# Value sums of a finished sequence placed among the scores of the next, and a layer's expert work cut into separate items

## The chip, the cores and the metric

The kernel runs on one core of one Trainium2 chip. The metric is device time in microseconds (us), the median of several executions of the same program. Inside the core the work is shared by TensorE (PE in the profile: matrix products and transposes), VectorE (DVE), ScalarE (ACT: exponentials, tanh, gelu, copies), GpSimd (POOL) and SyncE (SP: it issues the DMA transfers). Each engine takes its instructions strictly in the order in which the program gives them, and semaphores hold it where it needs another engine's result.

## The reference, cut to what matters

Four sequences of 512 tokens with 128 channels pass through four layers. Each layer normalizes x, computes a mixing branch s and a mixture of experts g from the normalized x, and adds `s * g` with g through a silu:

```python
x = L0_attn_x
for layer in (0, 1, 2, 3):
    xn = _layernorm(x, axis=-1)
    s = attn_ref(layer, xn)
    g = _silu(ffn_ref(layer, xn))
    x = x + s * g
```

The layers differ. Layer 0 is a selective scan with 8 experts. Layer 1 (the second layer, "causal") is causal attention with 16 heads of 8 channels, softmax with the row maximum taken out, and 4 gated experts that are ever used. Layer 2 (the third layer, "rope") is attention whose numerator uses rotated queries and keys and whose denominator uses the plain ones, so each score is computed twice, without maxima; its 8 experts have 64 hidden channels each. Layer 3 ("alibi") is attention with a distance bias and 16 routed experts. The change touches the order of work in layers 1 and 2.

## The kernel before, in words

`flow` builds one list of items for layers 1 to 3, written out as (what, layer, sequence, number). TensorE, ScalarE and VectorE all walk this list in `attention()` and do their own part of each item, so the list is the order on every one of them. SyncE has an order of its own, which the change leaves alone. The items are:

- `q`: one projection of the next sequence to queries or keys on TensorE, its copy out of the accumulator by ScalarE, and its split into three bf16 parts by VectorE (layer 2 has four of them); `v`: the values; `gate` and `cw`: the expert logits and, from them, the expert weights.
- `a`: a unit of scores (layers 1 and 3) of which VectorE takes the row maxima; `mx` turns the maxima, and SyncE writes them beside the queries.
- `b`: a unit of scores, 128 x 1024, of which ScalarE takes the exponential. Layer 1 has 20 of them a sequence, layer 2 has 64: 32 "plain" ones, whose exponentials are only summed (ScalarE takes two instructions of 512 columns, L1213), and 32 rotated ones (one instruction of 1024 columns, L1230). TensorE computes unit u when the exponential of unit u-2 is done, since the units share two pairs of accumulator banks.
- `pv`: one part of the value sums (L975), eight stages a sequence, each with one to three parts; the last part of four heads is followed by VectorE's copy (L1651), by `bc` (transposes on TensorE, L984, and the division by the denominator on VectorE, L1658).
- `f` in layer 1: an expert chunk. TensorE computes two products (`up`, L686 and L687), ScalarE a tanh (L1089), VectorE two products (`gated`, L1356 and L1360), and TensorE adds the chunk before it to the expert's output (`down`, L699). `up` of a chunk and all of `q`, `v`, `gate` and the transpose of `t` 3 use the accumulator bank MI, and each waits until the one before it has been read (`mi_read`).
- `f` in layer 2: `up` of two experts at once (L687), a gelu on ScalarE (L1094, with a table load before it and one behind it), and `down` of the chunk before it, which is two experts: the second expert's matmuls wait until VectorE (`mix`, L1382, four instructions) has read the first expert's output, since both use bank YB. `fl` is the last `down`; `mb` begins the mixture with the experts' biases (L666, L670).
- `t` 0 to 3, the tail of a sequence: transposes of the heads' output and ScalarE's copy (`t` 0, L990, L1248), the output projection (`t` 1, L996), VectorE's normalization, the combination with the experts and the next moments (`t` 2, L1678 to L1394), and the normalized x, its transpose (L651) and copy (`t` 3).

`schedule` gives a sequence's own items. In layer 1 it spreads the 22 expert chunks over `a` and `b`, and ends with the last value sums, the last chunk and `fl`; in layer 2 the last chunk and `fl` stand together before the last 16 items, and the last value sums stand at the end. `flow` then puts the tail of the previous sequence behind the items at `TAIL_AT` and the head items of the next sequence (`q`, `v`, `gate`, `cw`) behind those at `HEAD_AT`. So the end of one sequence of layer 2 and the beginning of the next read before:

```
... f3 fl b53 b54 b55 b56 b57 pv6.0 b58 pv6.1 b59 ... b63 pv7.0 pv7.1 bc3 |
    b0 b1 t0 b2 b3 t1 b4 b5 b6 t2 b7 ... b10 t3 b11 mb b12 b13 f0 pv0.0 b14 pv0.1 ...
```

Of the kernel before, what the change touches and what calls it, by code (L numbers as in the profile page):

```python
# [27 lines left out]
NB = 4  # L28
# [289 lines left out]
KIND = {1: "causal", 2: "rope", 3: "alibi"}  # L318
# [31 lines left out]
def schedule(l):  # L350
# [10 lines left out]
    a = [("a", u) for u in range(len(score_units(KIND[l])[0]))]  # L361
    b = b_items(KIND[l])
    if l == 1:
        return spread(a, f[:7]) + [("mx", 0)] + f[7:9] + spread(b, f[9:]) + [("fl", 0)]
    if l == 2:
        return b[:12] + [("mb", 0)] + b[12:14] + f[:1] + spread(b[14:-16], f[1:]) + [("fl", 0)] + b[-16:]
    return a + [("mx", 0)] + b
# [3 lines left out]

TAIL_AT = {1: (1, 4, 32, 47), 2: (1, 3, 6, 10), 3: (1, 3, 6)}
HEAD_AT = {1: (("q", 0, 36), ("q", 1, 40), ("v", 0, 44), ("gate", 0, 49), ("cw", 0, 52)),
           2: (("q", 0, 30), ("q", 1, 36), ("q", 2, 42), ("q", 3, 48), ("v", 0, 54), ("gate", 0, 58), ("cw", 0, 62)),
           3: (("q", 0, 8), ("q", 1, 12), ("v", 0, 16))}

# [5 lines left out]

def flow(layers):


    out, tail = [], []
    for l in layers:
        if not l:
            continue
        if l == 3:  # L390
            out += tail + [("route", l, 0, 0)]
            tail = []
        if l != 2 or l == layers[0]:
            out += tail + head_items(l, 0)
            tail = []
        for b in range(NB):
            after = {}
            for k, item in enumerate(tail):
                after.setdefault(TAIL_AT[l][k], []).append(item)
            if b + 1 < NB:  # L400
                for what, n, at_ in HEAD_AT[l]:
                    after.setdefault(at_, []).append((what, l, b + 1, n))
            elif l == 1 and 2 in layers:
                for k, item in enumerate(head_items(2, 0)):
                    after.setdefault(42 + 5 * k, []).append(item)
            for k, (what, n) in enumerate(schedule(l)):
                out.append((what, l, b, n))
                out += after.pop(k, [])
            assert not after, after
            tail = [("t", l, b, k) for k in range(len(TAIL_AT[l]) - (l == layers[-1] and l != 3))]  # L410
    return out + tail
# [1538 lines left out]
```

## Time and profile before

| | us |
|---|---|
| median of 3 executions | 2229.74 (2228.86 to 2235.36) |
| the profiled execution: its own time | 2235.12 |
| its span, first to last instruction | 2233.3 |
| TensorE busy | 1588.4 (71%) |
| VectorE busy | 1234.8 (55%) |
| ScalarE busy | 1040.8 (47%) |
| granted TensorE clock, mean share of full speed | 0.786 |

The second layer runs from about 625 to 1160 us of the span, the third from 1160 to about 1690, the fourth from there to the end. Busy shares are means over these stages, so they say little; what counts in a stage is which engine waits for which. TensorE's clock has two levels, 1.2 and 2.4 GHz, and a granted clock of 0.67 over a stretch means that it stood at the upper level for about a third of it.

### The profile page before, as it was taken

The page shows a single profiled execution, that of the slowest core. Times are in us where ns is not written, and L with a number is a line of the kernel's source. Part 1 is how long each engine was busy: PE and PEld are TensorE (multiplying, and loading weights), DVE is VectorE, ACT ScalarE, POOL GpSimd, SP SyncE. Part 2 cuts the span into 40 slices and gives each one's busy share as a digit, 9 for nine tenths or more (in the row PEclk, how much of TensorE's full clock was granted, in tenths as well). Part 3 has the DMA queues.
Part 4 walks back from the last instruction along what each step waited for, and adds up shares of the span by engine and source line. Part 5 has one row for each costly group of instructions (what it writes and reads, how often), then busy time and mean ns, then how long its engine had stood idle before and what let it go on. Part 6 is the DMA issues. An engine that isn't in the chain of part 4 may idle for free.

```text
span 2233.3 us, 24309 instructions
## 1 busy us (share of the span) xinstructions
PE 1588.4 (71%) x8520; PEld 786.7 (35%) x8520; DVE 1234.8 (55%) x2493; ACT 1040.8 (47%) x1569; POOL 222.0 (10%) x208
## 2 busy tenths in 40 slices
PE   5667657757679889797877767676674456877767
PEld 2444434434435445454442322222223042222222
DVE  4976958859765564746653324232215727455371
ACT  3856937748404133231336676576660031423415
POOL 0431413404200000000000000000000210000000
PEclk8987978878779999999996667576666575868768
DMA  5000000000111010010133203021001141111200
GB/s 220 1 1 0 0 0 0 0 0 0 35 55 52 8 44 15 2 50 8 30 86 111 71 17 97 15 78 36 1 1 43 39 113 41 55 41 37 56 22 6
DMA packets 73990, 83.09 MB, mean 37 GB/s; under 512 B 8764, under 2 KB 70716, under 8 KB 73276
## 3 DMA queue, kind: packets, MB, share of 16 engines
q1 hardware_dynamic: 72856, 79.60, 11.9%
q0 software_dynamic: 1024, 2.10, 0.3%
q8 instruction: 59, 0.97, 0.2%
q14 instruction: 51, 0.42, 0.1%
HBM read 50.47 MB, written 31.20 MB: 37 GB/s over the span
## 4 chain that ended last, share of the span: by engine, by line
PE 42%; DVE 29%; ACT 12%; issue 12%; DMA 2%; POOL 1%; SPq 1%; DVEq 0%; ACTq 0%; POOLq 0%
PE ps L975 9%; DVE neg_max L1638 7%; PE ps L699 6%; PE ps L687 5%; PE ps L686 4%; ACT scratch L1230 4%; DVE mixture_sum L1382 3%; ACT ps L1213 2%; DVE scratch L1486 2%; PE ps L845 2%; DVE gated L1356 2%; DVE hidden L1360 2%; PE ps L984 1%; DVE scratch L1475 1%; ACT tanh L1089 1%
## 5 line engine op out<-in xcount | busy, mean ns | idle before, releaser
L1230 ACT ACTIVATE scratch<-ps 128x1024 f32<-128x1024 f32 x336 | 335.2, 1021 | 290.1 <-PE ps L945 142.3
L1638 DVE TENSOR_REDUCE neg_max<-ps 128x2 f32<-128x1024 f32 (+2 forms) x224 | 224.5, 1064 | 20.8 <-PE ps L890 20.4
L975 PE MATMUL ps<-scratch,values 128*32 128x512 f32 (+3 forms) x1536 | 224.8, 671 | 15.7 <-ACT scratch L1230 10.1
L1651 DVE COPY head_out<-ps 128x512 f32<-128x512 f32 x48 | 33.1, 689 | 323.7 <-PE ps L975 323.6
L1811 POOL TENSOR_TENSOR scratch<-scratch 128x512 f32<-128x512 f32 x128 | 160.2, 1273 | 360.6 <-DVE scratch L1486 360.6
L1089 ACT ACTIVATE tanh<-ps 128x512 f32<-128x512 f32 x88 | 52.6, 597 | 291.9 <-PE ps L687 291.9
L699 PEld LDWEIGHTS ps<-weights_even,hidden 128*128 128x128 f32 (+1 forms) x960 | 148.0, 226 | 96.5 <-issue 53.7
L1213 ACT ACTIVATE ps<-ps 128x512 f32<-128x512 f32 x256 | 150.7, 589 | 63.9 <-PE ps L934 63.9
L699 PE MATMUL ps<-weights_even,hidden 128*128 128x128 f32 (+1 forms) x960 | 156.2, 315 | 33.5 <-DVE mixture_sum L1382 33.5
L1481 DVE TENSOR_TENSOR_SCAN scratch<-scratch 128x512 f32<-128x512 f32 x128 | 175.6, 1410 | 1.5 <-ACT scratch L1149 1.5
L687 PE MATMUL ps<-xnt_sequence,weights_even 128*128 128x512 f32 x256 | 149.5, 674 | 0.0
L1356 DVE SCALAR_TENSOR_TENSOR gated<-tanh,ps 128x512 f32<-128x512 f32 x88 | 60.4, 686 | 156.9 <-ACT tanh L1089 156.9
L1382 DVE SCALAR_TENSOR_TENSOR mixture_sum<-ps,combine,mixture_sum 128x128 f32<-128x128 f32 x304 | 85.2, 341 | 106.8 <-PE ps L699 106.8
L1094 ACT ACT_TABLE_LOAD x84 | 107.8, 1283 | 20.4 <-PE ps L699 19.0
L686 PE MATMUL ps<-xnt,weights_odd 128*128 128x512 f32 x176 | 107.9, 697 | 12.8 <-DVE hidden L1360 8.7
L1766 POOL TENSOR_SCALAR variance_eps<-mean_var 128x4 f32<-128x4 f32 x20 | 4.6, 228 | 1129.7 <-DVE mean_var L1279 1129.7
L750 PE MATMUL ps<-scratch 96*128 96x512 bf16 x128 | 42.7, 423 | 90.7 <-DVE scratch L1486 88.0
L699 PEld LDWEIGHTS ps<-weights_odd,hidden 128*128 128x128 f32 x640 | 87.4, 198 | 46.4 <-issue 40.7
L890 PE MATMUL ps<-scratch 52*128 52x256 bf16 (+7 forms) x704 | 103.6, 367 | 0.0
L934 PE MATMUL ps<-scratch 48*128 48x512 bf16 x256 | 72.6, 510 | 39.3 <-ACT ps L1213 38.4
L943 PE MATMUL ps<-scratch 48*128 48x512 bf16 x256 | 69.7, 517 | 41.6 <-ACT scratch L1230 34.8
L687 PE MATMUL ps<-xnt,weights_odd 128*128 128x512 f32 x176 | 97.7, 639 | 0.0
(268 smaller groups left out, 2545.4 us busy)
## 6 DMA issues: line engine op xcount, KB each, us to landing
scratch<-parts_scratch SPq DMA_DIRECT2D x288, 96.0 KB, 2.3
parts_scratch<-weights_even SPq DMA_DIRECT2D x192, 128.0 KB, 2.4
weights_odd<-in_l SPq DMA_DIRECT2D x1, 4224.0 KB, 28.2
weights_even<-in_l SPq DMA_DIRECT2D x1, 4096.0 KB, 17.2
weights_odd<-in_l SPq DMA_DIRECT2D x1, 4096.0 KB, 12.7
slots_scratch<-weights_even SPq DMA_DIRECT2D x2, 1280.0 KB, 6.3
scratch<-in_sel SPq DMA_DIRECT2D x1, 1024.0 KB, 6.4
slots_scratch<-xn SPq DMA_DIRECT2D x1, 1024.0 KB, 9.5
```

What stands on the lines that cost most here:

```text
L686: pe.matmul(ps[:, MI, :], W(l, "w3")[:, P * f:P * (f + 1)], src, start=True, stop=True)
L687: pe.matmul(ps[:, up_bank(l, f), :], w1, src, start=True, stop=True)\
L699: mm = pe.matmul(ps[:, YB, P * j:P * (j + 1)], buf[lo:lo + n, P * j:P * (j + 1)], W(l, "w2")[lo:lo + n, P * src:P * (src + 1)], start=(one ...
L975: mm = pe.matmul(ps[32 * i:32 * i + 32, PV, q0:q0 + n], lhs, buf[:, slot, col:col + n], start=first_, stop=True, skip_group_check=True)
L1094: act.activation(hidden_buffer(l, f), ps[:, up_bank(l, f), :], ACT.Gelu, bias=W(l, "b1")[:, f:f + 1])\
L1213: ins = act.activation(bank, bank, ACT.Exp, accum_out=dens[:, j, h:h + 1])
L1230: act.activation(dst, src, ACT.Exp).then_inc(q[l, "exp_done"], 1)
L1356: own.link(stt(act_g[:, :], act_t[:, :], 1.0, ps[:, UP, :], ALU.add, ALU.mult))
L1382: ins = stt(facc[:, j, :], yj, cw[:, j, e:e + 1], facc[:, j, :], ALU.mult, ALU.add)
L1481: dve.tensor_tensor_scan(l0["hs"][:, g, :], l0[f"da{s % 2}"][:, g, :], l0["ub"][:, g, :], 0.0, ALU.mult, ALU.add).then_inc(q[l, "da_free"], 1)
L1638: ins = dve.tensor_reduce(dst, ps[:, base:base + 2, col:col + n], AX.X, ALU.max, negate=True)
L1811: pool.tensor_tensor(l0["y"][:, g, :], l0["y"][:, g, :], l0["hc"][:, g, :], ALU.add)\
```

## The change

`schedule` no longer serves layers 1 and 2. New functions build each sequence:

- `split_late` takes the trailing `pv` and `bc` items off a sequence's list (layer 1: bc2, three parts of stage 6, stage 7, bc3; layer 2: stage 7 in two parts, bc3). `woven` puts them one at a time behind the first items of the next sequence, from its second item on, followed by `t` 0 and `t` 1 and, at distances filled with `None`, `t` 2 and `t` 3. This holds between the layers 1 and 2 too.
- In layer 1 the chunks 9 to 21 are spread over the shorter list, so they stand closer together, and the head items' places are counted in the new list.
- In layer 2 `mb` stands three items behind `t` 3, and each chunk gives three items, `f`, `dn` (f, 0) and `dn` (f, 1): the `up`, and each expert's `down` by itself with its `mix`. They are spread over the rest of the sequence.
- The items are the same in number and size but for that cut; the fourth layer's list is the same as before.

The same place in layer 2 reads after the change:

```
... b55 dn3.0 b56 b57 pv6.0 b58 dn3.1 pv6.1 b59 ... b63 |
    b0 b1 pv7.0 b2 pv7.1 b3 bc3 b4 t0 b5 t1 b6 ... b9 t2 b10 ... b13 t3 pv0.0 b14 pv0.1 mb b15 b16 b17
    pv1.0 b18 pv1.1 q0 f0 b19 bc0 b20 b21 b22 q1 dn0.0 b23 b24 b25 pv2.0 b26 q2 dn0.1 pv2.1 b27 ...
```

The middle of a sequence of layer 1, and its beginning, read before and after (x. marks items of the previous sequence, n. of the next):

```
before: mx f7 f8 b0 b1 b2 x.t2 b3 f9 b4 b5 n.q0 pv0.0 f10 b6 pv0.1 n.q1 b7 f11 pv0.2 b8 n.v pv1.0 f12 b9 x.t3
after:  mx f7 f8 b0 b1 b2 f9 b3 b4 x.t2 b5 f10 n.q0 pv0.0 b6 f11 pv0.1 n.q1 b7 pv0.2 f12 b8 n.v x.t3 pv1.0 b9 f13
before: bc2 pv6.0 pv6.1 f20 pv6.2 pv7.0 bc3 f21 fl | a0 a1 x.t0 a2 f0 a3 x.t1 a4 a5 f1
after:  f20 pv5.0 b19 f21 fl | a0 a1 x.bc2 a2 x.pv6.0 f0 x.pv6.1 a3 x.pv6.2 a4 x.pv7.0 a5 x.bc3 f1 x.t0 a6 x.t1
```

The diff, cut to its core:

```diff
-    if l == 1:
-        return spread(a, f[:7]) + [("mx", 0)] + f[7:9] + spread(b, f[9:]) + [("fl", 0)]
-    if l == 2:
-        return b[:12] + [("mb", 0)] + b[12:14] + f[:1] + spread(b[14:-16], f[1:]) + [("fl", 0)] + b[-16:]
-TAIL_AT = {1: (1, 4, 32, 47), 2: (1, 3, 6, 10), 3: (1, 3, 6)}
-HEAD_AT = {1: (("q", 0, 36), ("q", 1, 40), ("v", 0, 44), ("gate", 0, 49), ("cw", 0, 52)),
+def split_late(items):
+    n = len(items)
+    while items[n - 1][0] in ("pv", "bc"):
+        n -= 1
+    return items[:n], items[n:]
+def sequence1(b, late):
...
+    begin = spread(a, f[:7])
+    items, rest = split_late([(w, l, b, n) for w, n in b_items("causal")])
+    main = begin + [("mx", l, b, 0)] + f[7:9] + spread(items, f[9:]) + [("fl", l, b, 0)]
+    return woven(main, late, 1), rest
+def sequence2(b, late):
+    l = 2
+    items, rest = split_late([(w, l, b, n) for w, n in b_items("rope")])
+    items = woven(items, late + [None, None, ("mb", l, b, 0)], 1)
+    extra = []
+    for f in range(NF[l]):
+        extra += [("f", l, b, f), ("dn", l, b, (f, 0)), ("dn", l, b, (f, 1))]
+    first = items.index(("mb", l, b, 0)) + 2
+    return items[:first] + spread(items[first:-6], extra) + items[-6:], rest
+def woven(main, late, first):
+    late, out = list(late), []
+    for n, item in enumerate(main):
+        out.append(item)
+        if late and n >= first:
+            extra = late.pop(0)
+            out += [extra] if extra else []
+    return out + [item for item in late if item]
...
+HEAD_AT = {1: (("q", 0, 46), ("q", 1, 50), ("v", 0, 54), ("gate", 0, 59), ("cw", 0, 62)),
+           2: (("q", 0, 30), ("q", 1, 36), ("q", 2, 42), ("q", 3, 48), ("v", 0, 54), ("gate", 0, 60), ("cw", 0, 66)),
+def first_layers():
...
+            main, rest = (sequence1 if l == 1 else sequence2)(b, late)
...
+            t = [("t", l, b, k) for k in range(4)]
+            late = rest + ([t[0], t[1], None, None, None, t[2], None, None, None, t[3]] if l == 2 or b == NB - 1 else
+                           [t[0], t[1]] + [None] * 26 + [t[2]] + [None] * 9 + [t[3]])
...
-            def down(l, b, f):
+            def down(l, b, f, part=None):
...
-                for e, lo, n, src, one, last in DG[l][f]:
+                for e, lo, n, src, one, last in DG[l][f] if part is None else DG[l][f][part:part + 1]:
...
-                        if n:
+                        if l == 1 and n:
                             down(l, b, n - 1)
+                    elif what == "dn":
+                        down(l, b, n[0], n[1])
...
-            def mix(l, b, f):
+            def mix(l, b, f, part=None):
...
+                    elif what == "dn":
+                        mix(l, b, n[0], n[1])
```

## Rows read from the trace of the kernel before

**Rows 1.** The page: the span.

```profile
span 2233.3 us, 24309 instructions
```

**Rows 2.** Windows: a sequence of layer 1, one of layer 2.

```profile
core 0: us, PE busy (x) PEld busy (x) DVE busy (x) ACT busy (x) POOL busy (x), PEclk, DMA share, GB/s
760.00:895.00 135.00, 113.87 (x724) 62.64 (x722) 81.44 (x171) 36.18 (x48) 2.53 (x4) 0.95 0.09 25
...
1294.00:1424.00 130.00, 91.53 (x406) 33.87 (x406) 41.68 (x129) 87.22 (x183) 2.53 (x4) 0.68 0.17 49
```

**Rows 3.** Waits of ACT in 1290:1420, one sequence of layer 2: sum, times, longest.

```profile
ACT ps L1213 <- PE ps L934: 14.5, 9, 5.5
ACT scratch L1230 <- PE ps L943: 13.5, 6, 7.0
ACT xnt L1077 <- PE ps L651: 5.3, 1, 5.3
ACT weights_even L1200 <- PE ps L845: 4.5, 2, 3.7
ACT combine_second L1082 <- DVE combine L1314: 2.4, 1, 2.4
```

**Rows 4.** Timeline of ACT, layer 2: start, duration, in brackets the idle time before.

```profile
1318.69 1.94 ACT L1230 ACTIVATE scratch<-ps 128x1024 f32<-128x1024 f32 x2 [3.52 <-PE ps L943]
...
1403.12 1.02 ACT L1230 ACTIVATE scratch<-ps 128x1024 f32<-128x1024 f32 x1 [7.04 <-PE ps L943]
...
1423.32 0.58 ACT L1213 ACTIVATE ps<-ps 128x512 f32<-128x512 f32 x1 [6.21 <-PE ps L934]
```

**Rows 5.** Waits of PE in 1294:1424, layer 2.

```profile
PE ps L699 <- DVE mixture_sum L1382: 6.3, 5, 1.3
```

**Rows 6.** The page's costliest groups: the exponentials of the whole span.

```profile
L1230 ACT ACTIVATE scratch<-ps 128x1024 f32<-128x1024 f32 x336 | 335.2, 1021 | 290.1 <-PE ps L945 142.3
...
L1213 ACT ACTIVATE ps<-ps 128x512 f32<-128x512 f32 x256 | 150.7, 589 | 63.9 <-PE ps L934 63.9
```

**Rows 7.** Timeline of PE, layer 2, instructions at the upper clock.

```profile
1327.97 1.06 PE L975 MATMUL ps<-scratch,values 128*32 128x512 f32 x8
1328.96 0.39 PE L943 MATMUL ps<-scratch 48*128 48x512 bf16 x2
...
1391.38 1.12 PE L687 MATMUL ps<-xnt,weights_even 128*128 128x512 f32 x2
1392.43 1.16 PE L699 MATMUL ps<-weights_even,hidden 64*128 64x128 f32 x8
```

**Rows 8.** Timeline of PE, layer 2, instructions at the lower clock.

```profile
1316.04 2.07 PE L670 MATMUL ps<-weights_even,combine_t 8*128 8x128 f32 x8 [0.77 <-DVE combine_t L1348]
...
1365.79 2.08 PE L699 MATMUL ps<-weights_even,hidden 64*128 64x128 f32 x8
...
1405.48 0.61 PE L934 MATMUL ps<-scratch 48*128 48x512 bf16 x2 [0.59 <-ACT ps L1213]
1406.94 1.93 PE L975 MATMUL ps<-scratch,values 128*32 128x512 f32 x8
```

**Rows 9.** Waits of PE in 760:895, layer 1.

```profile
PE ps L873 <- DVE neg_max L1638: 6.7, 6, 1.9
...
PE ps L651 <- DVE branch L1292: 2.3, 1, 2.3
...
PE ps L984 <- DVE head_out L1651: 1.7, 2, 1.1
...
PE ps L975 <- DVE heads_out L1658: 1.4, 1, 1.4
```

**Rows 10.** Timelines of DVE and PE, layer 1: the tail's chain and a projection behind it.

```profile
806.06 1.11 DVE L1678 TENSOR_SCALAR branch<-branch,mean_var,rstd 128x128 f32<-128x128 f32 x4
...
812.88 0.65 DVE L1356 SCALAR_TENSOR_TENSOR gated<-tanh,ps 128x512 f32<-128x512 f32 x1
...
814.40 1.10 PE L845 MATMUL ps<-xnt,weights_odd 128*128 128x512 f32 x2 [2.36 <-DVE hidden L1360]
```

More of the change, by code:

```diff
@@ L360, in schedule @@
         return out + [("fl", 0)]
[L361 to L374 removed]
+    raise ValueError(l)
@@ new lines, in split_late @@
+def split_late(items):
[4 more added lines that the diff above has]
+def sequence1(b, late):
+    l = 1
+    f = [("f", l, b, n) for n in range(NF[l])]
+    a = [("a", l, b, u) for u in range(len(score_units("causal")[0]))]
+    begin = spread(a, f[:7])
+    items, rest = split_late([(w, l, b, n) for w, n in b_items("causal")])
+    main = begin + [("mx", l, b, 0)] + f[7:9] + spread(items, f[9:]) + [("fl", l, b, 0)]
+    return woven(main, late, 1), rest
@@ new lines, in with_extras, with sequence3 @@
+def with_extras(main, extras):
+    after = {}
+    for at_, item in extras:
+        after.setdefault(at_, []).append(item)
+    out = []
+    for n, item in enumerate(main):
+        out += [item] + after.pop(n, [])
+    assert not after, after
+    return out
+def sequence3(b):
+    a = [("a", 3, b, u) for u in range(len(score_units("alibi")[0]))]
+    return a + [("mx", 3, b, 0)] + [(w, 3, b, n) for w, n in b_items("alibi")]
+HEAD_AT = {1: (("q", 0, 46), ("q", 1, 50), ("v", 0, 54), ("gate", 0, 59), ("cw", 0, 62)),
+           2: (("q", 0, 30), ("q", 1, 36), ("q", 2, 42), ("q", 3, 48), ("v", 0, 54), ("gate", 0, 60), ("cw", 0, 66)),
@@ L375 @@
            3: (("q", 0, 8), ("q", 1, 12), ("v", 0, 16))}
+TAIL_AT = (1, 3, 6)
 def head_items(l, b):
     return [(what, l, b, n) for what, n, _ in HEAD_AT[l]]
-def flow(layers):
[L386 to L410, printed above, removed]
@@ new lines, in first_layers @@
+def first_layers():
+    out, late = head_items(1, 0), []
+    for l in (1, 2):
+        for b in range(NB):
+            main, rest = (sequence1 if l == 1 else sequence2)(b, late)
+            if b + 1 < NB:
+                extras = [(at_, (what, l, b + 1, n)) for what, n, at_ in HEAD_AT[l]]
+            elif l == 1:
+                extras = [(46 + 5 * k, item) for k, item in enumerate(head_items(2, 0))]
+            else:
+                extras = EXTRA3
+            out += with_extras(main, extras)
+            t = [("t", l, b, k) for k in range(4)]
+            late = rest + ([t[0], t[1], None, None, None, t[2], None, None, None, t[3]] if l == 2 or b == NB - 1 else
+                           [t[0], t[1]] + [None] * 26 + [t[2]] + [None] * 9 + [t[3]])
+    return out, late
@@ L411, in flow @@
+EXTRA3 = []
+def flow(layers):
+    out, late = first_layers()
+    out += [item for item in late if item] + [("route", 3, 0, 0)] + head_items(3, 0)
+    tail = []
+    for b in range(NB):
+        extras = list(zip(TAIL_AT, tail))
+        if b + 1 < NB:
+            extras += [(at_, (what, 3, b + 1, n)) for what, n, at_ in HEAD_AT[3]]
+        out += with_extras(sequence3(b), extras)
+        tail = [("t", 3, b, k) for k in range(3)]
     return out + tail
@@ L1360, in gated @@
                 stt(dst, act_g[:, :], 0.5, ps[:, MI, :], ALU.mult, ALU.mult).then_inc(q[l, "hidden_ready"], 1)
-            def mix(l, b, f):
+            def mix(l, b, f, part=None):
                 cw, facc = cws[b % 2 if l else 0], faccs[b % 2 if l else 0]
                 for n, (e, _, _, _, _, last) in enumerate(DG[l][f]):
-                    if not last:
+                    if not last or part not in (None, n):
                         continue
@@ L1708, in attention @@
                             gated(b, n)
-                        if n:
+                        if l == 1 and n:
                             mix(l, b, n - 1)
+                    elif what == "dn":
+                        mix(l, b, n[0], n[1])
                     elif what == "fl":
```

## The prediction, made before the changed kernel was run

> **What bounds the kernel now.** I read the page first: a span of 2233.3 us [rows 1], against 2235.1 us for that execution's own time and 2229.7 us for the median of the runs. The list of items changes only in the second and third layer, some 1065 us of the span, so I took a window of one sequence of each [rows 2], then the waits by engine in it [rows 3, 5, 9], then the timeline around the longest waits [rows 4, 7, 8, 10].
>
> Layer 1: TensorE is busy 114 of 135 us, at a granted clock of 0.95 [rows 2]. It is the bound. What it waits for is VectorE: 6.7 us for row maxima during the `a` units, 2.3 us for the normalized x, 1.7 and 1.4 us for the copy and the division at the ends of four heads [rows 9], and 2.4 us at a projection behind the tail's long chain [rows 10]. Moving work can win back only these few microseconds.
>
> Layer 2: no engine is the bound. In 130 us TensorE is busy 91.5 and ScalarE 87.2 [rows 2]. They work in turn, because only two score units are in flight. When TensorE has something long to do between two `b` units, ScalarE runs dry; between, TensorE waits for exponentials. The number to follow is ScalarE's idle time for TensorE, 14.5 + 13.5 + 5.3 + 4.5 + 2.4 us, with smaller waits 41 us a sequence [rows 3]. Three places make up most: 7.0 us where `f3` and `fl` stand together (two of four `down`s wait in turn for `mix`), 5.5 to 6.2 us at the sequence's end (pv7 and bc3 with no unit between), 5.3 us at the transpose of `t` 3 [rows 3, 4]. The bias products `mb` cost 3.5 us [rows 4]. TensorE itself waits 6.3 us for `mix` [rows 5].
>
> **The pace of an item in layer 2.** An exponential takes 1.02 us rotated, 2 x 0.59 us plain [rows 6]: 1.1 us a unit. TensorE's part of a unit takes 0.39 us at the upper clock and 0.61 at the lower [rows 7, 8]. A part of `pv` takes 1.06 or 1.93 us, an expert's `down` 1.16 or 2.08, `up` 1.12 and, by the same ratio, 2.08 [rows 7, 8]; a projection is `up`'s size. Let one such item of 2.0 us stand between two units at the lower clock. From the end of exponential u-2, TensorE needs 0.6 + 2.0 + 0.6 us and about 0.2 for the signal to have unit u+1 ready, while ScalarE has 2.2 us of work: it idles 1.2 us. At the upper clock the sum is 0.4 + 1.1 + 0.4 + 0.2 = 2.1 us and it idles nothing. Two items side by side idle it 1 to 3 us, three 2 to 4.7. So a place is cheap where single items alternate with units, and dear where the new list puts two or three side by side.
>
> **Layer 2, place by place**, ScalarE's idle time per sequence, before to after (the after values lie between what the rule above gives at the two clocks; where a range is given I take the value in front):
> - End and beginning: 5.5 before. After, pv7.0, pv7.1, bc3, t0, t1 alternate with b0 to b6. TensorE needs 8.1 us for them and 3 us for five units at the lower clock, ScalarE 6.6 us for its part: 4.6 idle; at the upper clock 0.5. I take 2.5.
> - `t` 3: one more unit between t1 and t3 (eight for seven) covers 1 us more of VectorE's chain: 5.3 to 4.3.
> - `mb`: 3.5 before, when the value sums pv0.0 and pv0.1 hid behind the gelu of f0. After, they stand bare behind t3, then `mb` with 2.07 us for the bias products, 1.0 for the transposes before them and the 0.77 us wait [rows 8]: 6.5 (4.5 to 7.2). This part loses 3.
> - q0 and f0 directly behind pv1.1: 3 (1.3 to 4.2), before 0.
> - The heart of the sequence, from q1 to pv6.1: before 7.0 + the `up`s, projections and the 2.4 us for the gates, 26.7 in all (41.0 less the three above). After: q1 with dn0.0 1, pv2.0 with its neighbours 0.9, q2 dn0.1 pv2.1 2, f1 q3 0.5, pv3.0 dn1.0 v 2.2, bc1 0.5, dn1.1 and gates 3, the eight items from f2 to pv5.1 2.5, from f3 to pv6.1 2.5: 15.1 (8 to 28).
> - Sum: 2.5 + 4.3 + 6.5 + 3 + 15.1 = 31.4 after, 41.0 before: -9.6, rounded to -9. From the two clocks' ends: 18.6 to 48.3 after, so -22 to +7.
> The third layer's last sequence keeps its end as it is (3 us less gain): 3 x 9 + 6 = -33 us. The waits for `mix` vanish as such: with three to five units between dn.0 and dn.1, its 1.1 us lies under exponentials; the number of gelu table loads does not change.
>
> **From layer 1 to layer 2.** Layer 1's last value sums, bc2, bc3, t0 and t1 (5 us of TensorE at the upper clock) now lie between plain units, where TensorE has 0.6 to 0.8 us spare each [rows 6, 7, 8], and their 2.4 us of waits vanish: -5.5 (0 to -8).
>
> **Layer 1.** At the three inner boundaries I followed the `a` units: pv6 and pv7 fill TensorE's waits for maxima, but VectorE gets the copy, two divisions and the last `mix` on top of the maxima and becomes nearly continuous; waits of about 5.7 us become 3.6: -2 each, -6. Against that the projections, values and gates now stand directly behind a chunk, and all use MI, so each waits for the chunk's tanh and two products, some 2.3 us less the `down` and whatever stands between. q0 is the worst: `t` 2 is a chain of 6.8 us on VectorE [rows 10], in front of chunk 10's products, and only b5 and f10 cover it, so the 2.36 us wait [rows 10] becomes about 4.3: +2. Values, gates, q1 and t3: +2. So +4 for the sequences 1 and 2, +2 for 3 (whose heads stood behind chunks already), +1 for 0: +11. Net +5 (-5 to +15). SyncE's list is the same; its stacks for the next sequence are late only if the queries are, and in layer 2 they come earlier.
>
> **Sum.** +5 - 5.5 - 33 = -33.5 us: 2235.1 becomes 2201.6, and the median 2229.7 becomes **2196 us**, 1.5% faster.
>
> **Rivals.**
> 1. *The clock rises and the third layer closes up* (0.25). With fewer holes TensorE is granted the upper level more often than the third of the time of rows 2. Layer 1, busy 84% of its time, shows 0.95; layer 2, busy 70%, shows 0.68 [rows 2]. On a line from -9 at 0.68 to -22 at 1.0, a clock of 0.85 gives -16 a sequence, 4 x -16 + 3 + 5 - 5.5 = -61.5: 2168 us. At 1.0 it is some -85. Against it: at the upper clock TensorE's busy share falls again. The Trainium skill, TensorE: Matmul & The Clock Gate, section What's actually happening, says that "the default state is throttled, and activity releases the throttle"; by that the clock would rise with the density that the new order brings, and the two rows agree in direction, though they cannot say where layer 2 would settle.
> 2. *The clock falls and the kernel is slower* (0.05). The new list spreads TensorE's work evenly instead of in bursts. If that keeps it at the lower level through layer 2, every single item costs 1.2 us and the neighbours more: up to +7 a sequence, 4 x 7 + 5 - 2 = +31: 2261 us. Break-even, on the line between the forecast at 0.68 and this at 0.5, is a mean clock of 0.59 in that layer. Against it: TensorE would then be busy nearly without a break, and in layer 1 that goes with the upper level.
> 3. *The gain is eaten in layer 1 and at `mb`* (0.13). If the two triples in layer 2 cost their lower-clock 4.7 and 4.5 us, -9 becomes -4, and the sum 5 - 5.5 - 13 = -13.5; if the crowded projections of layer 1 cost another 4 us in three sequences, it is -1.5: 2216 to 2228. For it: every crowded place named above. Against: TensorE's 6.3 us for `mix` and the 7.0 us hole go for certain.
> The forecast itself has 0.57, its own range -18 to -50: 2180 to 2212.
>
> **Range and chances.** 8 in 10 reaches from the middle of the first rival to the middle of the third: 2158 to 2221. A run of this kernel tells a difference from about 0.3%, 6.7 us. Faster by more: the forecast, rival 1, half of rival 3: 0.88. Within: 0.07. Slower: rival 2 without its mild end, 0.05.
>
> **What would show it.** In a window of a layer-2 sequence: about 121 us a sequence for 130; ACT's waits 31 for 41 us; no wait of L699 on L1382; no ACT wait over 5 us but the one on L651; a wait of over 5 us in front of the unit behind `mb`; table loads unchanged at 84. In layer 1: sequences 0 to 4 us longer, a PE wait of 4 us at L845 on L1360, less than 5 us for maxima. Wrong if the granted clock of layer 2 leaves 0.62 to 0.75, or if layer 1 moves by over 15 us.

## The result: 2236.8 us, no gain

In 20 runs of each kernel, taken in turns, the changed kernel's median is 2236.81 us (2232.12 to 2240.26), the one before's 2233.9 (2226.15 to 2236.66). The ratio is 1.0020 (95% interval 1.0011 to 1.0029): 0.2% slower, within the 0.3% that the prediction took as no change. It had said 2196 us and 0.07 for this outcome; the time is above its range. The kernel before has two levels among its 20 runs, nine at 2226.15 to 2229.74 us and eleven at 2233.85 to 2236.66; its profiled run is of the upper one, and the changed kernel's profiled run is its fastest.

The profile after: the span, and windows of one sequence of layer 1, one of layer 2, and all sequences of each; busy time by engine, then the granted clock.

```profile
span 2230.3 us, 24322 instructions
```

```profile
core 0: us, PE busy (x) PEld busy (x) DVE busy (x) ACT busy (x) POOL busy (x), PEclk, DMA share, GB/s
...
941.50:1081.50 140.00, 117.38 (x722) 63.07 (x720) 80.78 (x170) 35.94 (x48) 2.53 (x4) 0.93 0.08 24
...
1321.60:1448.60 127.00, 92.82 (x396) 36.04 (x397) 41.15 (x127) 86.96 (x180) 2.53 (x4) 0.66 0.18 50
...
670.70:1178.30 507.60, 428.25 (x2629) 231.90 (x2628) 288.04 (x613) 139.52 (x184) 7.59 (x12) 0.93 0.11 32
1178.30:1690.30 512.00, 361.30 (x1611) 135.99 (x1610) 160.67 (x501) 346.24 (x717) 12.64 (x20) 0.67 0.16 47
```

The same two stretches of the kernel before (from the first `mx` of layer 1 to layer 2's first exponential, and on to the last sequence's `t` 3):

```profile
670.40:1162.50 492.10, 418.24 (x2669) 231.44 (x2668) 290.26 (x618) 139.92 (x184) 7.58 (x12) 0.96 0.12 33
1162.50:1694.60 532.10, 366.32 (x1571) 134.70 (x1570) 159.25 (x496) 345.09 (x717) 12.64 (x20) 0.65 0.15 45
```

Layer 1 lost 15.5 us, layer 2 with the border won 20.1, and 1.6 more were lost elsewhere: 3.0 us less by the two profiled executions (2235.1 and 2232.1 us). That is not the sign of the medians, but both are far from the forecast's -33.5, which was +5 for layer 1 and -38.5 for layer 2 and the border.

**Layer 2.** ScalarE's waits in one sequence (sum, times, longest), then the timeline at their largest places:

```profile
ACT scratch L1290 <- PE ps L1001: 13.5, 7, 3.8
ACT ps L1273 <- PE ps L992: 11.4, 9, 5.1
ACT xnt L1137 <- PE ps L709: 5.8, 1, 5.8
ACT combine_second L1142 <- DVE combine L1374: 3.9, 1, 3.9
```

```profile
1324.92 1.02 ACT L1290 ACTIVATE scratch<-ps 128x1024 f32<-128x1024 f32 x1 [1.60 <-PE ps L1001]
1328.70 1.02 ACT L1290 ACTIVATE scratch<-ps 128x1024 f32<-128x1024 f32 x1 [2.75 <-PE ps L1001]
...
1355.72 1.02 ACT L1290 ACTIVATE scratch<-ps 128x1024 f32<-128x1024 f32 x1 [3.75 <-PE ps L1001]
...
1372.62 0.58 ACT L1273 ACTIVATE ps<-ps 128x512 f32<-128x512 f32 x1 [5.10 <-PE ps L992]
...
1382.18 0.24 ACT L1142 ACTIVATE combine_second<-combine 128x36 f32<-128x36 f32 x1 [3.94 <-DVE combine L1374]
...
1420.05 1.02 ACT L1290 ACTIVATE scratch<-ps 128x1024 f32<-128x1024 f32 x1 [2.83 <-PE ps L1001]
```

ScalarE idles 127.00 - 86.96 = 40.0 us a sequence. In the window of rows 2 it was 130.00 - 87.22 = 42.8, and 31 was forecast. The two holes of before [rows 3, 4] are gone, 7.0 us where `f3` and `fl` stood and 5.5 at the end, and so is TensorE's wait for `mix` [rows 5]. New ones have come. The largest shows why; TensorE's timeline ahead of it:

```profile
1366.10 1.94 PE L1033 MATMUL ps<-scratch,values 128*32 128x512 f32 x8
1367.96 2.07 PE L757 MATMUL ps<-weights_even,hidden 64*128 64x128 f32 x8
1369.97 2.07 PE L909 MATMUL ps<-weights_even,xnt 128*128 128x128 f32 x8
1371.97 0.61 PE L992 MATMUL ps<-scratch 48*128 48x512 bf16 x2
```

pv3.0, dn1.0 and v stand side by side, all at the lower clock: 5.9 us from the start of pv3.0 to the next score unit.

**Layer 1.** Its span grew by 15.5 us. TensorE's idle time grew by 5.5 of that (492.10 - 418.24 = 73.9 to 507.60 - 428.25 = 79.4), and its busy time by 10.0, with 40 matmuls fewer in the stretch (the last sequence's value sums now belong to layer 2): the same work at a clock of 0.93 instead of 0.96. From `mx` to `mx` the four stretches take 133.9, 137.0, 140.0 and 96.8 us, where they took 126.3, 135.8, 133.9 and 96.1. Waits of one sequence, to be read beside rows 9:

```profile
PE ps L931 <- DVE neg_max L1698: 4.2, 6, 1.3
PE ps L903 <- DVE hidden L1420: 3.8, 1, 3.8
PE ps L1033 <- DVE heads_out L1718: 2.8, 2, 1.6
```

The waits for maxima fell from 6.7 to 4.2 us, and q0 waits 3.8: as forecast. The clock was not in the forecast. Windows of 3 us in the last inner sequence, those at the lower level: first all of one such stretch and the start of the other before (of 134 us), then the four stretches after (of 140 us); busy time, then clock:

```profile
971.50:974.50 3.00, 2.73 (x15) 0.67 0.00 0
974.50:977.50 3.00, 3.00 (x6) 0.50 0.04 8
977.50:980.50 3.00, 3.00 (x20) 0.69 0.00 0
1034.50:1037.50 3.00, 1.48 (x14) 0.98 0.00 0
1037.50:1040.50 3.00, 1.71 (x9) 0.50 0.02 5
```

```profile
962.50:965.50 3.00, 1.91 (x2) 0.52 0.00 0
965.50:968.50 3.00, 3.00 (x17) 0.50 0.02 5
...
980.50:983.50 3.00, 0.45 (x4) 0.94 0.72 200
983.50:986.50 3.00, 3.00 (x21) 0.50 0.31 99
986.50:989.50 3.00, 3.00 (x6) 0.50 0.45 131
...
1013.50:1016.50 3.00, 3.00 (x10) 0.56 0.02 5
1061.50:1064.50 3.00, 3.00 (x5) 0.52 0.00 0
```

A stretch in which TensorE waits (0.45 us busy of 3) is followed by some six at 1.2 GHz in two of the four places and by some three in the others. There it is busy with hardly a break, and each matmul takes twice as long. So a wait of 2.55 us for `t` 3 has about three more lost behind it. TensorE's timeline at three of its waits:

```profile
963.59 1.19 PE L903 MATMUL ps<-xnt,weights_odd 128*128 128x512 f32 x1 [3.76 <-DVE hidden L1420]
...
983.34 1.08 PE L709 MATMUL ps<-consts,branch 128*128 128x128 f32 x4 [2.55 <-DVE branch L1352]
...
986.45 2.08 PE L744 MATMUL ps<-xnt,weights_odd 128*128 128x512 f32 x2
...
1013.45 1.61 PE L1033 MATMUL ps<-scratch,values 128*32 128x512 f32 x8 [1.64 <-DVE heads_out L1718]
```

The kernel before has such stretches too, one of them behind the same wait for `t` 3:

```profile
970.59 0.63 PE L651 MATMUL ps<-consts,branch 128*128 128x128 f32 x4 [2.27 <-DVE branch L1292]
```

But it has fewer. The ones behind q0's wait of 3.76 us and behind the 1.64 us for `heads_out` are new; before, a wait of 1.4 us for the same had none behind it. Before there are two in this sequence, some 14 us in all (each window's 3 us times twice what its clock lacks to 1.0), where the new list has four, some 20 us. At half speed those 7 us (6.8 unrounded) make some 3.5 of the 4.0 by which this sequence's busy time grew (113.34 to 117.38 us).

### The profile page after: what moved, and what is told of

It reads as the page before. It is cut to its first block, busy times and chain, and to the rows that moved or that the text cites. A ratio compares the mean times of both kernels' runs of the same rounds, so it can differ in the third digit from the quotient of the medians.

```text
span 2230.3 us, 24322 instructions
## 1 busy us (share of the span) xinstructions
PE 1600.1 (72%) x8520; PEld 791.4 (35%) x8520; DVE 1234.1 (55%) x2493; ACT 1041.5 (47%) x1569; POOL 222.0 (10%) x208
## 4 chain that ended last, share of the span: by engine, by line
PE 41%; DVE 28%; ACT 14%; issue 12%; DMA 2%; POOL 1%; SPq 1%; DVEq 0%; ACTq 0%; POOLq 0%
PE ps L1033 9%; DVE neg_max L1698 7%; PE ps L757 6%; PE ps L745 4%; PE ps L744 4%; ACT scratch L1290 4%; ACT ps L1273 3%; DVE mixture_sum L1442 2%; PE ps L903 2%; DVE scratch L1546 2%; DVE gated L1416 2%; DVE hidden L1420 2%; DVE scratch L1535 1%; ACT tanh L1149 1%; PE ps L792 1%
## 5 line engine op out<-in xcount | busy, mean ns | idle before, releaser
L1033 PE MATMUL ps<-scratch,values 128*32 128x512 f32 (+3 forms) x1536 | 236.2, 697 | 16.6 <-DVE heads_out L1718 10.5
L1698 DVE TENSOR_REDUCE neg_max<-ps 128x2 f32<-128x1024 f32 (+2 forms) x224 | 224.9, 1065 | 21.4 <-PE ps L948 21.2
L757 PEld LDWEIGHTS ps<-weights_even,hidden 128*128 128x128 f32 (+1 forms) x960 | 153.7, 231 | 67.6 <-issue 47.9
L1154 ACT ACT_TABLE_LOAD x84 | 107.8, 1283 | 21.3 <-PE ps L757 20.1
L992 PE MATMUL ps<-scratch 48*128 48x512 bf16 x256 | 69.9, 496 | 47.5 <-ACT ps L1273 46.6
```

Of the source, the lines that this page charges most:

```text
L757: mm = pe.matmul(ps[:, YB, P * j:P * (j + 1)], buf[lo:lo + n, P * j:P * (j + 1)], W(l, "w2")[lo:lo + n, P * src:P * (src + 1)], start=(one ...
L1033: mm = pe.matmul(ps[32 * i:32 * i + 32, PV, q0:q0 + n], lhs, buf[:, slot, col:col + n], start=first_, stop=True, skip_group_check=True)
L1154: act.activation(hidden_buffer(l, f), ps[:, up_bank(l, f), :], ACT.Gelu, bias=W(l, "b1")[:, f:f + 1])\
L1698: ins = dve.tensor_reduce(dst, ps[:, base:base + 2, col:col + n], AX.X, ALU.max, negate=True)
```

## The experiments

Fifteen kernels, in five groups. Each was timed in five rounds in turns with the kernel before, whose median was 2227.4, 2229.6, 2228.2, 2236.1 and 2229.5 us in the groups. "Difference" is what the ratio makes in us. Runs of different groups are compared by these ratios. In the group of h1 and h2 the kernel before was 7.8 us slower than in that of g4 to g6, so h1 is set against earlier runs by its ratio and by its median.

| run | layer 1 | layer 2 | median us | ratio (95%) | difference |
|---|---|---|---|---|---|
| e1 | new | old | 2251.67 | 1.0110 (1.0093-1.0126) | +24 |
| e2 | old | new | 2210.02 | 0.9923 (0.9904-0.9943) | -17 |
| e3 | old | woven, uncut | 2238.75 | 1.0049 (1.0034-1.0063) | +11 |
| e4 | old | cut, not woven | 2183.68 | 0.9805 (0.9790-0.9820) | -43 |
| f1 | woven only | old | 2241.94 | 1.0057 (1.0043-1.0070) | +13 |
| f2 | new, heads off the chunks | old | 2243.83 | 1.0074 (1.0055-1.0094) | +17 |
| f3 | old | e4, `t` 3 later | 2174.72 | 0.9761 (0.9747-0.9774) | -53 |
| f4 | old | new, `mb` before `t` 3 | 2190.39 | 0.9825 (0.9812-0.9839) | -39 |
| g4 | old | e4's places, woven | 2194.44 | 0.9841 (0.9824-0.9858) | -35 |
| g5 | old | g4, `t` 3 later | 2174.69 | 0.9754 (0.9738-0.9769) | -55 |
| g6 | old, border woven | g5 | 2170.27 | 0.9734 (0.9719-0.9749) | -59 |
| h1 | old | g5, gelu over value sums | 2165.53 | 0.9687 (0.9673-0.9700) | -70 |
| h2 | old, border woven | h1 | 2170.25 | 0.9697 (0.9681-0.9714) | -68 |
| i1 | old | h1, `mb` a unit later | 2157.51 | 0.9672 (0.9657-0.9686) | -73 |
| i2 | old | i1, `t` 2 a unit earlier | 2159.01 | 0.9687 (0.9672-0.9701) | -70 |

**Which layer: e1 and e2.** Each takes one layer's new list and leaves the other's old one.

```diff
 e1 +MODE1, MODE2 = 'new', 'old'
 e2 +MODE1, MODE2 = 'old', 'new'
```

> Only the second layer has the new order; the third keeps the old one, with each down written as two items at its old place (the same instructions in the same order), and the last value sums of the second layer stand at its end. Theory A (the second layer's new order is the loss: four or so us more of waits, and the rest because TensorE's matmuls there run at the lower clock more often, 0.93 for 0.96): slower than the kernel before by 8 to 18 us, a ratio of 1.004 to 1.008. Rival B (the second layer's loss in the trace is work handed over the border between the layers, or the clock of that one execution): within 4 us of the kernel before.

> Only the third layer has the new order; the second keeps the old one. Theory A: faster than the kernel before by 10 to 20 us, a ratio of 0.991 to 0.995. Rival B (what the third layer gained in the trace was only the second layer's tail handed over, or a lucky execution): within 5 us.

The new list costs 24 us in layer 1 and gives 17 in layer 2; the product of the ratios, 1.0032, is near the 1.0020 of the whole change. Part of e1's loss is its own: with layer 2's list old, layer 1's last value sums had to stand bare at its end. That stretch took 105.1 us, where it took 96.1 before and 96.8 after the change. Less these 9, 15 us remain, near the 15.5 of the trace.

So that the product fits is partly luck: 15 lost and 17 won make -2 us, and the whole change is 4.5 slower, though it has the border as well. Where the rest lies is seen in layer 2. Its new list, but for the border, took 127.0 and 126.6 us a sequence in the changed kernel, and in e2 less, at a higher clock:

```profile
1305.90:1430.10 124.20, 86.76 (x397) 32.97 (x397) 41.04 (x127) 87.00 (x180) 2.53 (x4) 0.72 0.18 51
1430.10:1553.10 123.00, 85.74 (x397) 33.58 (x398) 41.04 (x127) 86.91 (x180) 2.53 (x4) 0.72 0.19 52
```

**Which part of layer 2: e3 and e4.** e3 has the woven value sums with `f` and `down`s in one piece as before, e4 the three separate items with tails, heads and value sums at their old places.

```diff
 e3 -        extra += [("f", l, b, f), ("dn", l, b, (f, 0)), ("dn", l, b, (f, 1))]
    +        extra.append([("f", l, b, f)] + ([("dn", l, b, (f - 1, 0)), ("dn", l, b, (f - 1, 1))] if f else []))
 e4 +        extra += [("f", l, b, k), ("dn", l, b, (k, 0)), ("dn", l, b, (k, 1))]
    -    return it[:12] + [("mb", l, b, 0)] + it[12:14] + f[:1] + spread(it[14:-16], f[1:]) + [("fl", l, b, 0)] + it[-16:]
    +    return it[:12] + [("mb", l, b, 0)] + it[12:14] + extra[:1] + spread(it[14:-16], extra[1:]) + it[-16:]
```

> Second layer old. Third layer: the last value sums and the tail stand among the next sequence's first units as in the change, but each chunk's up is followed at once by both experts' down of the chunk before, and the last chunk by its own as well, as in the kernel before. Theory G (downs directly behind an up run under the gelu and its two table loads, so cutting them apart gives that cover away and wins little): as fast as the full new third layer or faster, 10 to 20 us below the kernel before. Rival S (the cut is what gains, since it removes the 7 us hole at the last chunk): only 3 to 8 us below it.

> Second layer old. Third layer: value sums and tail at their old places, only the experts cut into up, down, down and spread over the sequence (the head items' places are stretched with the list). Theory G: within 6 us of the kernel before, since the hole of 7 us at the last chunk goes and 2 to 4 us of idle TensorE under each gelu come. Rival S: 12 to 25 us faster.

The cut is worth 43 us alone, more than either theory allowed; weaving costs 11 without it, where both had a gain, and 26 on top of it. The theory that the `down`s were the gelus' cover and must not leave it falls. The 11 are not weaving by itself: e3's list also has new crowds, such as f1, dn0.0, dn0.1, v and pv3.1 between b34 and b35. A window of e4, and ScalarE's waits in it:

```profile
1295.04:1411.08 116.04, 83.30 (x397) 31.86 (x397) 40.66 (x127) 86.44 (x180) 2.53 (x4) 0.71 0.19 55
```

```profile
ACT ps L1324 <- PE ps L1043: 11.2, 7, 6.2
ACT xnt L1188 <- PE ps L760: 5.9, 1, 5.9
ACT scratch L1341 <- PE ps L1052: 5.8, 3, 3.5
```

ScalarE idles 116.04 - 86.44 = 29.6 us, 13 less than in rows 2 and 10 less than the old list at e1's higher clock (39.7, shown at the end), though the sequence's end (6.2), `t` 3 (5.9) and `mb` (3.5) cost what they did.

**Layer 1: f1 and f2.** f1 weaves the value sums, t0 and t1 of the first three sequences and leaves heads, t2, t3 and the chunks at the old places, but for f19 to f21, which now stand together at the end. f2 is e1 with queries, values and gates one to two items earlier, in front of a chunk for behind it.

```diff
 f1 +    cut = names.index(("bc", 2))
    +    rest = [item for item in main[cut:] if item[0] in ("pv", "bc")]
 f2 -HEAD_AT = {1: (("q", 0, 46), ("q", 1, 50), ("v", 0, 54), ("gate", 0, 59), ("cw", 0, 62)),
    +HEAD_AT = {1: (("q", 0, 45), ("q", 1, 49), ("v", 0, 52), ("gate", 0, 57), ("cw", 0, 60)),
```

> Third layer old. Second layer: the value sums bc2 to bc3 of sequences 0 to 2 and t0, t1 stand among the next sequence's first a units as in the change, but chunks, projections and t2, t3 keep their old places (only f19 to f21 now stand together at the end, since the value sums between them are gone); the last sequence is old. Theory C (the loss sits where the chunks and projections are crowded in the middle of a sequence, waits plus lower clock): within 5 us of the kernel before. Rival P (the placing of the value sums among the a units itself costs, through VectorE's queue and the clock there): 8 us or more slower.

> As the run with the new order in the second layer alone, but each projection, the values and the gates stand in front of the chunk behind which they stood, so that none waits for a chunk's products in bank MI; t3 moves with the values. Theory C: 6 to 14 us faster than that run, so 10 to 18 us slower than the kernel before. Rival P: within 4 us of that run, some 24 us slower than before.

Weaving alone costs 13 us, with no projection moved; that is rival P's figure. The window of one sequence of f1:

```profile
799.80:939.70 139.90, 119.00 (x722) 64.52 (x722) 80.88 (x170) 36.16 (x48) 2.53 (x4) 0.91 0.09 24
```

TensorE is idle 20.9 us. The same sequence before takes 135.80 us with 114.37 busy at 0.95, idle 21.4. The 4 us are lost in busy time alone. Over the whole of layer 1, f1 takes 505.2 us for 492.1, with 429.58 busy for 418.24: 11.3 of the 13.1 us are busy time. The old list shows no such spread. In twelve of the thirteen profiles that have it, the first three stretches agree within 0.2 us; h1 alone is faster, by 0.7 to 2.2 us each. f2 is 8 us faster than e1, as theory C had it, though the two intervals touch: the heads' places account for some 8 us of e1's loss.

**Places in layer 2: f3, f4.** f3 is e4 with `t` 3 two units later, behind `mb`; f4 is e2 with `mb` in front of `t` 3, which stands two units later.

```diff
 f3 -OLD_TAIL = {2: (1, 3, 6, 10)}
    +OLD_TAIL = {2: (1, 3, 6, 13)}
 f4 -    items = woven(items, late + [None, None, ("mb", l, b, 0)], 1)
    +    items = woven(items, late[:-1] + [("mb", l, b, 0), None] + late[-1:], 1)
    -                late = rest + ([t[0], t[1], None, None, None, t[2], None, None, None, t[3]] if nxt == 2 else
    +                late = rest + ([t[0], t[1], None, None, None, t[2], None, None, None, None, None, t[3]] if nxt == 2 else
```

> Second layer old, third layer with only the experts cut, and in it t3 three units later, behind the bias products instead of in front. In the run with the cut alone TensorE and ScalarE both stand 5.9 us a sequence at t3, for VectorE's chain that begins at t1. If that wait is real time on the path: 4 to 6 us a sequence less than that run, in all 15 to 24 us, so about 2160 to 2170 us where the kernel before has 2227. If the time only moves (bias products bare before it): within 5 us of that run.

> Second layer old. Third layer as the change has it, value sums woven and experts cut, but the bias products one unit in front of t3 and t3 two units later, which also gives the twelve expert items three more units to stand between. If the combination of both parts loses against the cut alone because bias products, value sums and expert items crowd behind t3: faster than the new third layer by 15 us or more, at or below the run with the cut alone (2184). If woven value sums cost by themselves: 8 to 12 us faster than the new third layer through t3 alone, about 2200.

Both gain: f3 10 us on e4, between the two cases expected, and f4 22 on e2, still 4 short of e4. The 5.9 us wait for `t` 3's transpose, which only waits for VectorE's chain, is 1.9 in f3's second sequence; 4.3 had been forecast for the change, which left it at 5.8.

```profile
1295.07 0.60 ACT L1188 ACTIVATE xnt<-ps 128x512 f32<-128x512 f32 x1 [1.88 <-PE ps L760]
```

**Weaving without crowding: g4, g5, g6.** The expert items and heads stand at e4's units, except that `mb` and the first `up` stand two units later (b13 and b15) and `t` 3 behind b12, and the value sums are woven too (`tail[2]` and `tail[3]` are t2 and `t` 3, `u` the unit just put out). g6 also hands the value sums of layer 1's last sequence to layer 2, with t2, `mb` and `t` 3 three units later in that one.

```diff
 g4 +    behind = dict(zip((15, 16, 19, 23, 27, 31, 34, 38, 42, 46, 50, 52), expert))
    +        if u == 9:
    +            out.append(tail[2])
    +        if u == 13:
    +            out.append(("mb", l, b, 0))
    +        if u == 12:
    +            out.append(tail[3])
 g5 -        if u == 12:
    +        if u == 14:
 g6 +    shift = 3 if b == 0 else 0
    +                if l == 1 and b == NB - 1:
    +                    rest = [item for item in main[cut:] if item[0] in ("pv", "bc")]
```

> Layer 1 as before. Third layer: experts in three items each, and up to unit 63 every expert item, projection and mb at the unit where e4 (cut alone, span 2181.2 us, 115.6 us a sequence, ScalarE waits 29 us a sequence, 6.2 us of them at the sequence's end) has it; in addition the last value sums, bc3, t0 and t1 stand among the next sequence's first units, t2 behind unit 9, t3 behind unit 12. If weaving pays and only the crowding behind t3 and mb cost in the changed kernel, most of the 6.2 us at the end goes, 3 to 4 us in three sequences: a span near 2170. If weaving itself costs (TensorE loses the dense stretch at the end, or mb and t3 now stand bare), the span is 2181 or more and the waits at mb and t3 grow by what the end gives back.

> As the run g4, with t3 behind unit 14, past mb: it stands to f3 (cut alone with t3 three units later, span 2171.7 us) as g4 stands to e4. If weaving pays: 2160 to 2165. If weaving costs by itself: 2172 or more. If the place of t3 is what cost (its transpose waits for VectorE's chain), g5 is faster than g4 by 2 to 3 us a sequence, 8 to 10 us in all.

> As the run g5, and at the border from layer 1 to layer 2 too: the last value sums of layer 1's last sequence stand among the third layer's first units, as the prediction priced at -5.5 us, with t2, mb and t3 three units later there. If that price holds: 4 to 6 us below g5. If the units of the start get crowded as in the changed kernel: equal to g5 or slower.

Against e2, g4 wins 18 us: that is the crowding, `mb` and `t` 3 having moved by a unit or so only. Against e4 it loses 8, and g5 is level with f3: weaving still gives nothing. g6 is 4.5 us faster than g5, near the 5.5 predicted for the border, but the two intervals overlap. Where the 6.2 us of the end go is seen in g4's timeline behind `mb`:

```profile
1310.53 1.02 ACT L1360 ACTIVATE scratch<-ps 128x1024 f32<-128x1024 f32 x1 [5.38 <-PE ps L1071]
...
1312.94 1.02 ACT L1360 ACTIVATE scratch<-ps 128x1024 f32<-128x1024 f32 x1 [1.38 <-PE ps L1071]
```

The units behind `mb` are 6.8 us late; in e4 it is 3.5. In e4 the first `up` stands in front of pv0.0, so pv0.0 and pv0.1 run while ScalarE is in the table loads and the gelu. In g4, as in the changed kernel, they stand bare in front of `f0`.

**The first gelu over the value sums: h1 and h2.** h1 is g5 with `mb` behind unit 11, `t` 3 behind unit 15 and the first `up` directly in front of pv0.0; h2 adds the border, as g6 did.

```diff
 h1 -        if u == 13:
    +        if u == 11:
     ...
    -        if u == 14:
    +        if u == 15:
     ...
    +    first = expert[0]
    +    out.remove(first)
    +    out.insert(next(i for i, item in enumerate(out) if item[0] == "pv" and item[2] == b), first)
 h2 +    shift = 2 if b == 0 else 0
```

> As the run g5 (third layer cut, value sums woven, span 2178.8 us), with one thing changed behind the boundary: mb behind unit 11 and the first expert's up product directly in front of the first value sums, as in the cut-only list, so that they lie under its gelu; t3 behind unit 15. Theory K (what weaving gives back at mb is the cover that the first gelu gave the first value sums): ScalarE's wait at mb falls from 6.2 + 1.7 us to about 3.5, 3 to 4 us a sequence, and the span comes to 2163 to 2168. Theory L (TensorE simply has that much work between t0 and unit 16, and where it stands doesn't matter): the wait moves to another place there, and the span stays at 2175 to 2181.

> As the run h1, with layer 1's last value sums among the third layer's first units too (as g6 to g5, where it gave 9.2 us of span and 4.4 us of the median). Adding up: 4 to 6 us below h1, and the fastest kernel of the study if theory K holds, near 2160; near 2170 under theory L.

h1 gains 15 us on g5 by the ratios and 9 by the medians (2174.7 to 2165.5). Its span, 2161.8 us, is a little under theory K's 2163 to 2168, but 4.0 us of the 17.0 between the two spans lie in layer 1, which is the same in both. Against f3, weaving is now worth 17 us by the ratios and 9 by the medians, so with the cover kept it pays (`t` 3 stands three units later than in f3). But K's detail missed: the wait at `mb` stays at 6.2 us, and only those behind it went (1.7 us in g5). h1 moved `mb`, `t` 3 and the `up` at once; no run separates them. h2's border adds nothing to h1: there the first sequence's t2, `mb` and `t` 3 moved too. The wait has another cause. Timelines of VectorE and TensorE in h1:

```profile
1278.48 0.69 DVE L1800 TENSOR_TENSOR branch<-ps,xn 128x512 f32<-128x512 f32 x1 [3.67 <-PE ps L1127]
...
1288.53 0.65 DVE L1481 COPY combine_t<-ps 8x512 f32<-8x512 f32 x1
```

```profile
1289.23 2.07 PE L801 MATMUL ps<-weights_even,combine_t 8*128 8x128 f32 x8 [4.19 <-DVE combine_t L1481]
```

`mb`'s transposes were done at 1285.0, but the copy that its products need stands in VectorE's queue behind the whole chain of t2. Before the change, t2 stood three units earlier and this wait was 0.77 us. In h2's first sequence t2 stands only one unit ahead of `mb`, and the wait is the longest of all:

```profile
1182.54 2.07 PE L805 MATMUL ps<-weights_even,combine_t 8*128 8x128 f32 x8 [7.29 <-DVE combine_t L1485]
```

**VectorE's queue at mb: i1 and i2.** i1 is h1 with `mb` a unit later; i2 is i1 with t2 a unit earlier.

```diff
 i1 -        if u == 11:
    +        if u == 12:
 i2 -        if u == 9:
    +        if u == 8:
```

> As the run h1 (span 2161.8 us) with mb behind unit 12 for 11. In h1 TensorE waits 4.19 us for VectorE's copy of the gates' transpose, which stands in VectorE's queue behind the whole chain of t 2 (from 1280.4 to 1288.6 us), and ScalarE waits 6.19 us for the unit behind it; in g5, with mb behind unit 13, the wait for the copy is 1.85 us. If that queue is the cause: about 3 us for the copy, ScalarE's wait near 5, 1 us a sequence less, a span of 2157 to 2161. If it is only that so much TensorE work stands there: ScalarE's wait stays at 6, span 2161 to 2165.

> As the run i1, and t 2 behind unit 8 for 9, so that VectorE has one unit more to finish its chain before the copy for mb. If VectorE's queue is the cause: the wait for the copy falls to 2 us or less, ScalarE's wait at mb to 3.5 to 4, a span of 2153 to 2158. If t 2 is then itself waited for, it gives that back and stays level with i1.

In i1 the wait for the copy falls from 4.2 to 2.8 us and ScalarE's from 6.2 to 5.3, as expected for the queue:

```profile
1292.55 2.07 PE L801 MATMUL ps<-weights_even,combine_t 8*128 8x128 f32 x8 [2.76 <-DVE combine_t L1481]
```

But at like clocks little of that reaches the sequence's time. The windows of i1's second sequence (109.16 us, shown at the end) and of h1's third, both at 0.75, differ by 0.2 us:

```profile
1410.48:1519.84 109.36, 81.98 (x399) 30.93 (x397) 40.57 (x127) 86.66 (x180) 2.53 (x4) 0.75 0.21 58
```

i1 is the fastest kernel of the study, 2157.51 us or 3.3% under the kernel before, though its interval overlaps h1's. i2 missed what it was built for: the wait falls from 1.82 to 0.92 us in the first sequence and is still 2.76 in the three others. VectorE's chain starts when t1's product ends and then runs through; where t2's item stands in the list does not set it.

## Why the prediction was wrong

**Layer 1, "Net +5 (-5 to +15)": its waits were sized rightly in sum, and its clock was left out.** Idle time grew by 5.5 us against +5 forecast, and q0's wait of 3.8 us is near the predicted 4.3. The other 10.0 us are busy time at the lower clock. The step that failed was to price a moved item in layer 1 by its wait alone and to let the granted clock stand at 0.95. The text applied a falling clock to layer 2 only, in the second rival. f1 shows that weaving by itself does it: equal idle time, clock 0.91. Why equal idle time in other places costs more clock is not settled. In the changed kernel's sequence each lower stretch stands behind a wait, and there are more separate ones than before, but no run here varied the holes one at a time. Part of it is not the list's at all: the changed kernel's second stretch takes 137.0 us at 0.95, and the same list in e1, with nothing different ahead of it, 140.2 at 0.93, both with TensorE idle 22.5 to 22.6 us. The Trainium skill (TensorE: Matmul & The Clock Gate, What's actually happening) says that activity releases the throttle. The 3 us windows agree, with 0.45 us busy ahead of a stretch at 0.50. The mean doesn't show it: f1's TensorE is busy 119.00 of 139.90 us, the same share as the old list's 114.37 of 135.80, at a lower clock.

**Layer 2, "-9 per sequence": the rule held at its lower clock, and the value taken from it was wrong.** The forecast put ScalarE's idle time at 31.4 us, and it is 40.0. By place:

- End and beginning: no wait over 1 us is left, as predicted.
- `t` 3: 5.8 us for 4.3. One unit more didn't shorten it.
- `mb`: 1.60 + 2.75 us for 6.5. In the first sequence the unit behind `mb` waits 5.45 us, in the others 2.75 to 3.73.
- From q0 on: 18.1 forecast. With some 2.3 for the boundary, 40.0 - 2.3 - 5.8 - 4.4 = 27.5 measured. Four places hold 3.75 + 5.10 + 3.94 + 2.83 = 15.6 of it. They are those at which the text had q2 dn0.1 pv2.1 (2), pv3.0 dn1.0 v (2.2), dn1.1 and gates (3) and f3 to pv6.1 (2.5): 9.7. Before, the same reckoning leaves 42.8 - 5.5 - 5.3 - 3.5 = 28.5 us for this part, so it hardly changed, where the prediction had it fall by 8.6.

The rule's own arithmetic with three items at the lower clock gives 0.6 + 6.1 + 0.6 + 0.2 - 2.2 = 5.3 us for the place of pv3.0, dn1.0 and v, and 5.10 was measured; the prediction's "three 2 to 4.7" is its own rule summed half a microsecond low. The step that failed is the choice of a value between the two clocks, as if a place had a mean clock. TensorE is at one level or the other, and at the two triples it was at the lower. That was rival 3's condition ("if the two triples cost their lower-clock 4.7 and 4.5 us"; 5.10 and 3.75 were measured), which got 0.13. With layer 1's cost added, the outcome lies beyond even that rival. How much of the 40.0 us is the list's is less certain. In e2 the same list idles ScalarE 37.2 and 36.1 us at a clock of 0.72, against 39.7 of the old list at 0.72 in e1: at like clocks it wins 2.5 to 3.6 us a sequence, still not 9.

**The cut and the weaving were priced as one.** The text saw gains from both. Alone the cut gives 43 us, more than the forecast for everything. Weaving takes 26 of them away again (e2 against e4): 18 by crowding (e2 against g4) and 8 that remain without the crowding (g4 against e4). Of what is behind those 8, the prediction saw that pv0.0 and pv0.1 stand bare, and priced it at 3 us a sequence. It did not see that the first `up` in front of them is their cover (9 to 15 us from g5 to h1, with `mb` and `t` 3 moved along), nor that `t` 3 had better go behind `mb` (10 us in f3, 19 from g4 to g5). VectorE's queue is not among the causes in the changed kernel, where `mb` stands late and waits 0.77 us for its copy, as before; it is what g5, h1 and i1 pay for placing `mb` nearer to t2.

**The border** at -5.5 us: g6 against g5 gives 4.5 in the ratio, with overlapping intervals, and h2 against h1 gives nothing, so its worth is not shown.

**Right:** no wait for `mix`, table loads still 84, layer 2's clock at 0.66 to 0.69, q0's wait. **Wrong:** 121 us a sequence (127.0), waits of 31 (40), no ACT wait over 5 us but the one on `t` 3 (5.10 at L992), over 5 us in front of the unit behind `mb` (in one sequence of four only). Layer 1 moved by 15.5 us, which the text had named as a sign of error.

## What to carry to other kernels

Where two engines work in turn, price a moved item by its neighbours at the lower clock, and keep single items between units: a cut into small pieces pays (43 us here), and moving other work into the gaps that it needs takes the gain back (26). Before work leaves the cover of a long activation, or a chain is moved later, ask what stood beside it: the cheapest repairs here were one `up` in front of two value sums with `mb` and `t` 3 moved along (9 to 15 us) and a transpose placed behind the product that needn't wait for it (10 us). Test the parts of a change one at a time; this one was a gain of 43 us, hidden under two losses.

## What the runs showed of the hardware that was not expected

- The same list runs at two granted clocks. Layer 2's old list takes 130.0 us at 0.68 in rows 2, and in e1, where only layer 1 differs, 126.30 us at 0.72, with ScalarE idle 39.7 us for 42.8. It happens within one run too: h1's second and third sequence of layer 2 have one list and take 112.43 us at 0.71 and 109.36 at 0.75. The window of e1:

```profile
1332.68:1458.98 126.30, 85.90 (x396) 32.86 (x397) 41.13 (x127) 86.61 (x180) 2.54 (x4) 0.72 0.18 51
```

  Why it differs was not tried. Differences of some 3 us a sequence between two profiled executions are therefore not read here as an effect of a list; the table's ratios are.
- In layer 2 a closer order went with a clock only a little higher: 0.66 to 0.72 with the changed list (in its own profile and in e2's), 0.71 in e4 at 116 us a sequence, 0.75 in i1's second and third sequence at 109, but 0.68 in its first at 113. From the changed kernel to i1 TensorE's busy time falls with it, from 92.8 to 82.4 us a sequence:

```profile
1301.19:1410.35 109.16, 82.44 (x398) 30.97 (x396) 40.55 (x127) 86.64 (x180) 2.53 (x4) 0.75 0.21 58
```

  ScalarE's idle time fell by as much as the sequence did, from 40.0 to 22.5 us (109.16 - 86.64). That is the direction of rival 1, a clock that rises and a layer that closes up, but with single items in the gaps, which this change didn't have. Since one list alone spans 0.66 to 0.72, the runs do not show that the closer order is what raised the clock.
